# Local attention: score sums in column strips, queries in SBUF, and a share of the products on GpSimd

## The reference

```python
q = (x @ WQ_w + WQ_b).reshape(Bx, Lx, nh, d)          # nh = 16 heads, d = 64
k = (x @ WK_w + WK_b).reshape(Bx, Lx, nh, d)
ak = (ax @ WK_w + WK_b).reshape(Bx, 1, nh, d)         # ax: one condition vector per sequence
av = (ax @ WV_w + WV_b).reshape(Bx, 1, nh, d)
pad_k = jnp.pad(k, ((0, 0), (1, 1), (0, 0), (0, 0)))
k_shift = jnp.stack([pad_k[:, t:Lx + t] for t in range(3)], axis=3)
K = concatenate([akb, k_shift], axis=3); V = concatenate([avb, k_shift], axis=3)
scores = jnp.einsum('blhd,blhjd->blhj', q, K) / jnp.sqrt(jnp.float32(d))
alphas = jax.nn.softmax(scores, axis=-1)              # over 4 places
att = jnp.einsum('blhj,blhjd->blhd', alphas, V).reshape(Bx, Lx, nh * d)
return att @ WO_w + WO_b
```

## Time and profile before

| | us |
|---|---|
| median of 3 runs | 2283.66 |
| lowest and highest run | 2279.72, 2284.48 |
| span of the profiled execution, first to last instruction | 2274.4 |
| local attention within it | 701 to 1084 |
| mean granted TensorE clock, share of full speed | 0.945 |

### The profile page before, as it was taken

How to read it: one execution, slowest core, us unless ns; L and a number is a source line. 1 busy time by engine, 2 the same in 40 slices (tenths; PEclk the granted TensorE clock), 3 DMA queues, 4 the chain that set the end, 5 groups by cost and what they waited for, 6 DMA issues and landing times.

```text
span 2274.4 us, 74250 instructions
## 1 busy us (share of the span) xinstructions
PE 2000.1 (88%) x31569; PEld 1323.4 (58%) x31675; DVE 1705.3 (75%) x3808; ACT 1001.4 (44%) x2827; POOL 458.8 (20%) x793
## 2 busy tenths in 40 slices
PE   7888888998886888787799999985999789999998
PEld 5555534444454555553567677763666456677776
DVE  3444489999965878787888888843999668888887
ACT  2333236566652121221455555542554445555555
POOL 2211000000000434335012122243432112121200
PEclk9999699999978899898899999996999999999999
DMA  2000000000010000000311111106553211111111
GB/s 61 4 3 4 1 1 1 1 1 1 1 38 17 2 3 2 3 3 2 111 48 44 44 44 44 39 4 128 107 108 73 65 40 44 39 44 44 44 57 37
DMA packets 76083, 77.35 MB, mean 34 GB/s; under 512 B 15756, under 2 KB 57060, under 8 KB 74180
## 3 DMA queue, kind: packets, MB, share of 16 engines
q1 hardware_dynamic: 71848, 70.11, 12.1%
q10 hardware_dynamic: 3904, 2.49, 0.4%
HBM read 60.09 MB, written 11.82 MB: 32 GB/s over the span
## 4 chain that ended last, share of the span: by engine, by line
PE 24%; DVE 18%; ACT 6%; issue 5%; DMA 1%; ACTq 1%; SPq 1%; POOL 1%; another core or an unknown queue 0%; POOLq 0%; DVEq 0%
PE B L85 23%; DVE work L2097 4%; DVE hr L2061 3%; DVE work L2105 3%; DVE work L107 2%; ACT hr L103 2%; ACT ltc L103 2%; ACTq L2384 1%; ACT catt L103 1%; DVE lth L107 1%; DVE lh L107 1%; DVE lpq L107 1%; ACT work L103 1%; DVE gr L1911 1%; DVE work L1471 1%
## 5 line engine op out<-in xcount | busy, mean ns | idle before, releaser
L85 PE MATMUL B<-gr,wres 128*128 128x512 f32 x1248 | 353.3, 411 | 16.4 <-DVE work L2105 10.2
L103 ACT ACTIVATE work<-B 128x512 f32<-128x512 f32 (+5 forms) x460 | 233.3, 524 | 124.4 <-PE B L85 69.3
L2147 POOL COPY G<-lh 128x32 f32<-128x32 f32 x256 | 148.2, 579 | 680.3 <-DVE lh L107 680.3
L85 PE MATMUL B<-work 128*128 128x128 bf16 (+3 forms) x1408 | 259.6, 312 | 28.3 <-ACT work L103 7.0
L85 PEld LDWEIGHTS B<-gr,wres 128*128 128x128 f32 x1248 | 214.2, 189 | 83.4 <-DVE work L2105 27.8
L103 ACT ACTIVATE hr<-work 128x512 fp32r<-128x512 f32 x272 | 172.9, 636 | 146.6 <-DVE work L2105 76.7
L85 PEld LDWEIGHTS B<-work 128*128 128x128 bf16 (+2 forms) x1408 | 141.3, 127 | 138.8 <-issue 79.5
L2061 DVE TENSOR_TENSOR hr<-work,hr 128x512 fp32r<-128x512 f32 x272 | 186.5, 686 | 8.1 <-ACT hr L103 6.6
L2097 DVE TENSOR_TENSOR work<-work 128x512 f32<-128x512 f32 x256 | 178.7, 698 | 14.0 <-ACT work L103 6.6
L107 DVE SCALAR_TENSOR_TENSOR work<-work,cw 128x512 f32<-128x512 f32 x240 | 179.2, 746 | 5.9
L85 PE MATMUL B<-hr,wres 128*128 128x512 f32 x624 | 177.9, 394 | 1.0 <-DVE hr L2061 1.0
(11 more groups left out here) (254 smaller groups left out, 3790.2 us busy)
## 6 DMA issues: line engine op xcount, KB each, us to landing
work<-wdr SPq DMA_DIRECT2D x128, 256.0 KB, 3.1
scr<-catt SPq DMA_DIRECT2D x144, 64.0 KB
work<-scr SPq DMA_DIRECT2D x16, 384.0 KB
work<-scr SPq DMA_DIRECT2D x16, 192.0 KB
catt<-in_L_ffn_ew SPq DMA_DIRECT2D x24, 128.0 KB, 2.4
work<-scr SPq DMA_DIRECT2D x16, 128.0 KB
out<-work SPq DMA_DIRECT2D x32, 64.0 KB, 2.2
work<-in_x ACTq DMA_DIRECT2D x2, 512.0 KB, 5.3
```

The lines of the kernel that those rows point to most:

```text
L85: return e.matmul(out, lhsT, rhs, start=start, stop=stop, skip_group_check=True)
L103: return e.activation(out, in_, func, bias=bias, scale=scale)
L2147: e.tensor_copy(self.G[:, :, t], self.lh[:, t % 4, :]).then_inc(*inc("l.pool", "h", li, t))
```

## The change

Scores are now summed the other way round: a selector of 128x32 (`selh[:, c, :]`, ones in columns 2c and 2c+1 for the two heads) is the stationary operand and the product of 128x512 is streamed. The three places j write the column strips 32j to 32j+31 of bank `Bs`, summed over the eight chunks in PSUM; the condition's term goes to partitions 96 to 111. There are thus 3 matmuls a chunk in place of 48, and the scores have heads on the partitions, so that in the middle of a unit ScalarE copies 112x512 to SBUF (into `pr[0]`), TensorE transposes four blocks of 112x128, and only then ScalarE copies `sc` (the condition is now place 3, not 0). ScalarE also copies each query chunk with its bias to one of two SBUF buffers `q`; VectorE makes products 0 and 1 from it as plain `tensor_tensor`, GpSimd product 2. There are six `pr` buffers; the sixth and the `q` buffers lie in `spare`, which shares its place with `wr`. The ring's query bank is free after ScalarE's copy. A unit has 57 turns. `selh` is built on GpSimd where `blk` was. The core of the diff:

```diff
@@ late_constants_pool
-        then(e, sel(e, self.blk[:], self.ones[:, 0:2], ALU.is_ge, 0.0, 0, [[-64, 2]], 1), "const", "blk0")
-        sel(e, self.blk[:], self.blk[:], ALU.is_ge, 0.0, 63, [[64, 2]], -1).then_inc(*inc("const", "blk"))
+        then(e, e.memset(self.selh[:], 0.0), "const", "selh0")
+        for half in range(2):
+            r = slice(64 * half, 64 * half + 64)
+            then(e, sel(e, self.selh[r], self.selh[r], ALU.not_equal, 1.0, -half, [[-2, 8], [1, 32]], 0), "const", "selh", half)
@@ cond2_ring_free
-            name = ("cd%d.dve" % wk, "p", i, p // 2, 2) if p % 2 else ("cd%d.act" % wk, "k", i, p // 2)
+            name = ("cd%d.act" % wk, "q" if p % 2 else "k", i, p // 2)
@@ cond2_pe
             def scores(c):
+                e.wait_ge(*at(dve, "p", i, c, 1))
+                e.wait_ge(*at(f"cd{wk}.pool", "p", i, c))
                 for j in range(3):
-                    e.wait_ge(*at(dve, "p", i, c, j))
-                    for k in range(4):
-                        for r in range(0, 128, 32):
-                            last = mm(e, S3[r:r + 32, k, 2 * c:2 * c + 2, j + 1],
-                                      m["pr"][(3 * c + j) % 5][:, k * 128 + r:k * 128 + r + 32], self.blk[:], False, False)
-                    last.then_inc(*inc(pe, "s", i, c, j))
+                    last = mm(e, Bs[32 * j:32 * j + 32, :], self.selh[:, c, :], m["pr"][(3 * c + j) % 6], c == 0, c == 7)
+                last.then_inc(*inc(pe, "s", i, c))
...
             for k, b in enumerate(un):
-                for r in range(0, 128, 32):
-                    mm(e, S3[r:r + 32, k, :, 0], self.X[:, b, r:r + 32], self.Gak[:, b, :], k == 0, False)
+                mm(e, Bs[96:112, k * 128:k * 128 + 128], self.Gak[:, b, :], self.X[:, b, :], k == 0, True)
...
             scores(7)
-            for _ in range(4):
+            yield
+            yield
+            e.wait_ge(*at(a, "sT", i))
+            for k in range(4):
+                last = e.transpose(Bs[:, k * 128:k * 128 + 112], sT[0:112, k * 128:k * 128 + 128], self.ident[0:112, 0:112])
+            last.then_inc(*inc(pe, "st", i))
+            for _ in range(3):
                 yield
@@ cond2_act
+                e.wait_ge(*at(pe, "q", i, c))
+                if c >= 2 or i:
+                    old = (i, c - 2) if c >= 2 else (i - 1, c + 6)
+                    e.wait_ge(*at(f"cd{wk}.pool", "p", *old))
+                    e.wait_ge(*at(dve, "p", *old, 1))
+                act(e, m["q"][c % 2], Bq[:], ACT.Identity, bias=self.ckc[:, 0, c:c + 1]).then_inc(*inc(a, "q", i, c))
...
-            e.wait_ge(*at(pe, "s", i, 7, 2))
+            e.wait_ge(*at(pe, "s", i, 7))
+            act(e, m["pr"][0][0:112], Bs[0:112, :], ACT.Copy).then_inc(*inc(a, "sT", i))
+            yield
+            e.wait_ge(*at(pe, "st", i))
...
-            act(e, m["sc"], S3.rearrange("p b h j -> p (b h) j"), ACT.Copy).then_inc(*inc(a, "s", i))
+            act(e, m["sc"].rearrange("p (b h) j -> p b j h", b=4), S4, ACT.Copy).then_inc(*inc(a, "s", i))
@@ cond2_dve, product
                 if j == 0:
-                    e.wait_ge(*at(pe, "q", i, c))
-                    e.wait_ge(*at(a, "k", i, c))
-                if n >= 5:
-                    e.wait_ge(*at(pe, "s", i, (n - 5) // 3, (n - 5) % 3))
+                    e.wait_ge(*at(a, "q", i, c))
+                if n >= 6:
+                    e.wait_ge(*at(pe, "s", i, (n - 6) // 3))
...
-                stt(e, four(pr[n % 5]), four(Bq[:]), self.ckc[:, 0, c:c + 1], KP[:, c, :, j:j + 128], ALU.add,
-                    ALU.mult).then_inc(*inc(dve, "p", i, c, j))
+                e.tensor_tensor(four(pr[n % 6]), four(m["q"][c % 2]), KP[:, c, :, j:j + 128], ALU.mult).then_inc(
+                    *inc(dve, "p", i, c, j))
             for c in range(8):
-                if c:
-                    product(c - 1, 2)
                 yield
                 product(c, 0)
                 yield
                 product(c, 1)
                 yield
-            product(7, 2)
+            yield
@@ cond2_pool
         for i in range(4):
-            for _ in range(29):
-                yield
             for c in range(8):
                 yield
                 yield
+                e.wait_ge(*at(f"cd{wk}.act", "q", i, c))
+                if c >= 2:
+                    e.wait_ge(*at(pe, "s", i, c - 2))
+                elif i and c == 0:
+                    e.wait_ge(*self.cond2_att(wk, i - 1, 7))
+                e.tensor_tensor(four(pr[(3 * c + 2) % 6]), four(m["q"][c % 2]), KP[:, c, :, 2:130], ALU.mult).then_inc(
+                    *inc(f"cd{wk}.pool", "p", i, c))
+                yield
+            for _ in range(6):
+                yield
```

More of the change, by code:

```diff
@@ L171, in __init__ @@
         self.bank = [ctx.enter_context(nc.psum_tensor(f"B{i}", [128, 512], F32)) for i in range(8)]
+        with nc.sbuf_tensor("spare", [128, 3072], F32) as self.spare:
+            pass
         self.wr = [[sb(f"wr{i}{j}", [128, 768], F32R) for j in range(2)] for i in range(2)]
@@ L272, in lay_constants @@
         self.condT2 = sb("condT2", [128, 32])
-        self.blk = sb("blk", [128, 2])
+        self.selh = sb("selh", [128, 8, 32])
         self.selc = sb("selc", [128, 16, 64], BF16)
@@ L1081, in lay_cond2 @@
         for wk in range(2):
-            self.cd.append({"KP": ar(128, 8, 4, 130), "pr": [ar(128, 512) for _ in range(5)], "sc": ar(128, 64, 4),
+            self.cd.append({"KP": ar(128, 8, 4, 130), "pr": [ar(128, 512) for _ in range(5)] + [self.spare[:, 1536 * wk:1536 * wk + 512]],
+                            "q": [self.spare[:, 1536 * wk + x:1536 * wk + x + 512] for x in (512, 1024)], "sc": ar(128, 64, 4),
                             "m": ar(128, 64), "sm": ar(128, 64), "R": ar(128, 64, 4),
@@ L1255, in cond2_pe @@
         Bs = self.bank[3 * wk + 2]
-        S3 = Bs[:, 0:256].rearrange("p (b h j) -> p b h j", b=4, h=16)
+        sT = m["pr"][0]
         for _ in range(COND2_LAG * wk):
@@ L1261, in cond2_pe @@
         e.wait_ge(*at("cprep.dve", "w", 1, 1))
-        e.wait_ge(*at("const", "blk"))
+        e.wait_ge(*at("const", "selh", 1))
         for i in range(4):
@@ L1299, in cond2_pe @@
             for k in range(4):
-                last = e.transpose(Bs[0:16, k * 128:k * 128 + 128], Sv[:, k, 0, :], self.ident[:])
+                last = e.transpose(Bs[0:16, k * 128:k * 128 + 128], Sv[:, k, 3, :], self.ident[:])
             last.then_inc(*inc(pe, "a0", i))
@@ L1345, in cond2_act @@
         Bs = self.bank[3 * wk + 2]
-        S3 = Bs[:, 0:256].rearrange("p (b h j) -> p b h j", b=4, h=16)
+        S4 = Bs[:].rearrange("p (b j x) -> p b j x", b=4, j=4)[:, :, :, 0:16]
         for _ in range(COND2_LAG * wk):
@@ L1358, in cond2_act @@
             for c in range(8):
-                Bk = self.cond2_ring(wk, 43 * i + 2 * c)
+                Bk, Bq = self.cond2_ring(wk, 43 * i + 2 * c), self.cond2_ring(wk, 43 * i + 2 * c + 1)
                 e.wait_ge(*at(pe, "k", i, c))
@@ L1404, in cond2_dve @@
         Rv = R.rearrange("p x y -> p (x y)").rearrange("p (b j h) -> p b j h", b=4, j=4)
-        S3, R3 = Sv[:, :, 1:4, :], Rv[:, :, 1:4, :]
+        S3, R3 = Sv[:, :, 0:3, :], Rv[:, :, 0:3, :]
         for _ in range(COND2_LAG * wk):
@@ L1417, in product @@
             def product(c, j):
[L1418 removed]
+                n = 3 * c + j
                 if j == 0:
[L1420 to L1423 removed]
+                    e.wait_ge(*at(a, "q", i, c))
+                if n >= 6:
+                    e.wait_ge(*at(pe, "s", i, (n - 6) // 3))
                 elif i and n == 0:
                     e.wait_ge(*self.cond2_att(wk, i - 1, 7))
[L1426 to L1427 removed]
+                e.tensor_tensor(four(pr[n % 6]), four(m["q"][c % 2]), KP[:, c, :, j:j + 128], ALU.mult).then_inc(
+                    *inc(dve, "p", i, c, j))
             for c in range(8):
[L1429 to L1430 removed]
                 yield
@@ L1440, in cond2_dve @@
             e.wait_ge(*at(a, "s", i))
-            then(e, e.tensor_tensor(S4[:, :, :, 0], S4[:, :, :, 0], self.cak[:, un[0]:un[0] + 4, :], ALU.add), dve, "s0", i)
+            then(e, e.tensor_tensor(S4[:, :, :, 3], S4[:, :, :, 3], self.cak[:, un[0]:un[0] + 4, :], ALU.add), dve, "s0", i)
             then(e, red(e, m["m"], sc, ALU.max), dve, "m", i)
@@ L1464, in cond2_dve @@
                     e.wait_ge(*at(pe, "b", i, c, j))
[L1465 to L1468, removed]
-                    else:
-                        e.wait_ge(*self.cond2_att(wk, i, (n - 29) // 3))
-                    e.tensor_tensor(four(pr[n % 5]), four(B[:]), KP[:, c, :, j:j + 128], ALU.mult).then_inc(
+                    if n < 30:
+                        e.wait_ge(*at(pe, "s", i, (n - 6) // 3))
+                    elif n % 3 < 2:
+                        e.wait_ge(*at(f"cd{wk}.pool", i, (n - 30) // 3))
+                    else:
+                        e.wait_ge(*self.cond2_att(wk, i, (n - 30) // 3))
```

(12 more changed lines are left out.)

## The result

The changed kernel takes 2344.01 us (median of 4 runs, 2342.48 to 2352.22) against 2281.69 for the kernel before in the same job: ratio 1.0276, 95% interval 1.0252 to 1.0299. It is slower by some 62 us; the span grew from 2274.4 to 2340.8 us.

A forecast was written before the change was run, and what follows sets the result against it. VectorE, closely followed by TensorE, was taken to bound local attention. Exclusion 25 + middle 12 + key-side term 1 - lone steps 6 + selectors 0.5 = +32 us on 2283.7 gave 2316 us, range 2275 to 2353.

The forecast's parts named there:

- the exclusion: Overlapping steps: VectorE instructions with two SBUF operands and GpSimd's tensor-tensor ones take turns; 5.05 against 4.42 us, +25 us.
- The signs named for it: Local attention: SBUF products at 1.0 us or more, GpSimd up to 1.8, value products 0.68, six sum records within 1.1.
- its own mechanism: Local attention: some form of the forecast's exclusion makes the kernel slower, 2295 to 2340 us; 66%.
- the wide range: Whole kernel: 2275 to 2353 us, leaving out 17%.
- rival 3: Overlapping steps: the order of the queues makes GpSimd's product wait for ScalarE; steps of 5.7 us, +65, 2349 us; 10%.
- The sum over heads: TensorE in a step: three column strips run together in 0.9 us, nothing gained or lost (+0.05 a step).
- ScalarE's copy: Query copies in the steps: 64 of 0.69 us, 44 us covered by ScalarE's idle time, costed at 0.
- its cover: GpSimd in a step: three instructions take 3.84 us, which alone still fits in 4.42.
- The middle: Middle of each of 8 units: added copy, transposes and softmax meeting GpSimd, 1.5 us each, +12 us, from 0 to +28.
- lone steps: 24 score steps alone or beside a softmax: 0.25 us gained in each, -6 us, from 0 to -19.
- time around the span: Whole kernel: runs stand 5 to 10 us above the profiled span (median 9.3), taken as lying around it and untouched.

The follow-up runs named there:

- e6: Changed kernel with only the strips, sixth buffer and longer middle kept: no query copy, VectorE makes all three products from PSUM; 2287.2 us.
- e4: Changed kernel with VectorE's two products of a chunk one turn later in its queue; 2322.2 us.
- e2: Changed kernel with VectorE's two products reading the query from its PSUM bank again, still waiting for ScalarE's copy; 2324.5 us.
- e9: Changed kernel with the edits of e2 and e5 together, and VectorE's products one turn later; 2286.0 us.
- e12: e9 with the second worker 24 turns behind instead of 22; 2314.9 us.
- e5: Changed kernel with worker 1's memsets, and their wait, 20 turns later in GpSimd's queue; 2337.1 us.

## Why the prediction was right, and what it undersized

Direction and mechanism held: slower, through the exclusion of VectorE's SBUF products and GpSimd. The signs named for it came too: SBUF products at 1017 ns, GpSimd's products at 1510 to 1650, value products still at 0.68, six sum records in 1.06 us. The size was about half (32 of 62 us). The prediction gave its own mechanism 2295 to 2340 us, and 2344 lies outside that; only the wide range, which reached to 2353 and took in most of rival 3, held the time. A second cause of much the same size stood beside the forecast one and wasn't in it: that the range held is luck in part.

- The sum over heads: costed at 0.9 us and nothing gained or lost; 0.89, and e6 confirms it.
- ScalarE's copy: costed at 0, and this is the term that failed. I asked whether ScalarE had time (it had) and who is queued behind ScalarE's wait, but not who is queued behind the one who waits for the copy. The key copy and the query copy stand one behind the other, so the product starts 0.7 us later than when it read PSUM, on an engine whose queue also holds the other worker's value products, for which TensorE waits. Covering part of the wait gave 22 us in e4 and 32 between e2 and e9, with the doubt said at e12.
- The exclusion: costed at 5.05 - 4.42 = 0.63 us a step, 25 us. Taking it off the products gave 0.45 a step (5.50 to 5.05) and 19.5 us in e2, and 29 us with the products one turn later, so the term was about right. The step as a whole was forecast at 5.05 and measured 5.50, since the wait came on top. That e2's step is 5.05 too is chance: e2 has the wait and not the exclusion.
- GpSimd: its cover was taken from the steady steps. At the start of the stage its queue holds worker 1's memsets and their wait for a transfer; 6.9 us by e5. A queue has to be read from its beginning, not only in the steady part.
- The middle: VectorE's softmax now meets GpSimd in worker 0's units too. From the addition of the condition's term to the last cast it takes 52.4 us in all over 8 units instead of 46.3. One of them in order of time:

```profile
741.38 1.26 DVE L1456 TENSOR_TENSOR work<-work,catt 128x64 f32<-128x64 f32 x1
...
745.57 1.19 DVE L1466 CAST work<-work 128x192 bf16<-128x192 f32 x1
```

  That is (52.4 - 46.3) / 8 = 0.8 us a unit, as priced (0.78). Middle and lone steps together were given 12 - 6 = 6 us. In e9, whose steps are 0.10 shorter (40 x 0.10 = 4) and whose stage is still 7.9 longer, they come to 12; in the changed kernel 68 - 41 - 7 = 20 are left for them. How these split between the copy, the transposes and the lone steps wasn't measured. Part of it comes with the strips: the step of chunks 0 to 1 of worker 0's values, which isn't among the 30, takes 6.3 to 7.2 us in the changed kernel and 5.2 to 6.4 in e6 instead of 3.8 to 4.7, that of chunks 6 to 7 some 9.4 in both instead of 8.0 to 8.5.
- Rival 3, a step of 5.7 by the order of the queues at 2349 us, was the nearest in its numbers. It had the place wrong: it looked for the loss in GpSimd's queue, where e5 found 6.9 us, and the larger wait is in VectorE's.
- The prediction also set the span beside the runs' median and took the difference of 5 to 10 us for time around the span. The profiled run of the changed kernel took 2342.48 us with a span of 2340.8, so 1.7 us lie around it; the rest was the difference from run to run. The forecast time doesn't depend on it.

What stays open: a kernel with GpSimd's product in which VectorE reads the query's bank without waiting for the copy wasn't run, and it alone would price the wait; and the 29 us of e12.

## What to carry to other kernels

An operand moved from PSUM to SBUF isn't only a faster read (0.69 instead of 0.74 us here): if it makes a VectorE instruction read SBUF twice, that instruction and GpSimd's tensor-tensor instructions take turns (1.02 and 1.51 to 1.65 us here), and work "given to GpSimd" stops VectorE. A copy on an idle engine can cost its latency where an in-order queue waits for it at its head: look at what stands behind the one who waits, and try the consumer a turn later, measuring each place, since a shift of two turns between the workers was worth 29 us by itself. Before putting work into an idle queue, read that queue from its first instruction.

## What the runs showed of the hardware

GpSimd's product of four blocks of 128 columns, with VectorE's products reading PSUM (e2), took 1.18 to 1.21 us, less than its contiguous addition of the same size (1.28), so no cost of the pattern shows. The exclusion also holds for a VectorE cast from float32 to bf16 with one SBUF operand (L1466, 1.19 us here, 0.33 undisturbed) and for an instruction of only 64 columns (L1456, 1.26 us instead of 0.26), which lost more than the products of 512 columns did on average (0.33). The page "SBUF — State Buffer" of the Trainium skill ("SBUF: two separate sides") names two kinds of VectorE instruction that take turns with GpSimd, those with two SBUF inputs and those in a mode with two ports. For the first kind the trace agrees; whether the cast ran in such a mode no run shows.
